# First attention: a tile's value products in small pieces among the next tile's units, two places for probabilities, context loaded later

## What is computed

```python
qkv = x @ w_qkv                        # 16 heads of 64
q, k = rope(q), rope(k)
scores = q @ k.T / 8                   # (16, 512, 512), causal
kerple = -softplus(log_p) * log1p(softplus(log_a) * |i - j|)
hidden = gelu(concat(scores, kerple over heads) @ w1 + b1)      # 32 -> 32
scores = scores + kerple + hidden @ w2 + b2                     # 32 -> 16
weights = softmax(causal(scores))
out = (weights @ v) @ w_o
```

## Time and profile before

| | |
|---|---|
| median of 3 runs (lowest to highest) | 4395.63 us (4395.07 to 4396.11) |
| the profiled execution | 4399.94 us |
| its span, first to last instruction | 4398.2 us |
| PE / DVE / ACT busy in the span | 87% / 56% / 38% |
| share of the chain that ended last: PE / DVE / ACT | 66% / 16% / 7% |
| mean granted TensorE clock | 0.934 of full |

### The profile page before, as it was taken

One profiled execution on the slowest core, in us unless ns is written; L12 is line 12 of the kernel. 1 busy time (PEld: TensorE's weight loads), 2 busy tenths in 40 slices (PEclk: granted clock), 3 DMA queues, 4 the chain that ended last, 5 costly groups with the idle time before them and its releaser, 6 DMA issues.

```text
span 4398.2 us, 57319 instructions
## 1 busy us (share of the span) xinstructions
PE 3843.8 (87%) x21938; PEld 1843.6 (42%) x21938; DVE 2449.9 (56%) x6073; ACT 1681.6 (38%) x2508; POOL 152.0 (3%) x168
## 2 busy tenths in 40 slices
PE   5778888999977888899987798889998879888999
PEld 2342444345434244435533424443553442443355
DVE  5457566742356756673236575657324667665632
ACT  2644433431264542352136354235113636422511
POOL 1000020000000001000000001100000000200000
PEclk9998999999999998899998999889999889988999
DMA  5213002122421201202241210120315121012031
GB/s 191 96 31 60 17 18 48 22 87 75 129 75 37 45 17 42 45 1 101 65 161 44 41 36 17 42 45 1 105 61 161 49 45 27 18 42 45 1 112 59
DMA packets 134702, 254.40 MB, mean 58 GB/s; under 512 B 23268, under 2 KB 82660, under 8 KB 128996
## 3 DMA queue, kind: packets, MB, share of 16 engines
q1 hardware_dynamic: 134408, 250.50, 20.0%
HBM read 156.04 MB, written 44.04 MB: 45 GB/s over the span
## 4 chain that ended last, share of the span: by engine, by line
PE 66%; DVE 16%; ACT 7%; SPq 5%; issue 3%; DMA 2%; POOL 0%; DVEq 0%; POOLq 0%; ACTq 0%
PE ps L1207 11%; PE ps L578 7%; PE ps L1225 5%; DVE mx L732 5%; PE ps L561 5%; SPq L429 5%; PE ps L506 4%; PE ps L1543 3%; DVE ps L729 3%; PE ps L1461 3%; PE ps L402 3%; ACT a_X L1616 2%; PE ps L566 2%; PE ps L1485 2%; DMA a_fin<-scores 2%
## 5 line engine op out<-in xcount | busy, mean ns | idle before, releaser
L670 ACT ACTIVATE PT<-ps 128x1024 f32<-128x1024 f32 (+3 forms) x640 | 604.8, 958 | 473.1 <-PE ps L566 243.6
L506 PE MATMUL ps<-KS,QS 96*128 96x512 bf16 (+3 forms) x1280 | 469.3, 406 | 114.6 <-DVE mx L732 53.5
L732 DVE TENSOR_REDUCE mx<-ps 128x1 f32<-128x512 f32 (+3 forms) x768 | 437.8, 619 | 169.0 <-PE ps L506 82.7
L1207 PE MATMUL ps<-xnT,f_w 128*128 128x512 f32 x1088 | 490.9, 595 | 0.0
L561 PE MATMUL ps<-QS,KS 99*128 99x512 bf16 (+2 forms) x1280 | 429.7, 381 | 6.7 <-ACT QS L660 6.2
L729 DVE CUSTOM_DVE_ANT_0 ps<-ps,mneg 128x512 f32<-128x512 f32 x512 | 342.2, 715 | 133.0 <-PE ps L506 131.3
L578 PE MATMUL ps<-PT,VP 128*32 128x512 f32 (+3 forms) x2560 | 386.5, 588 | 14.2 <-ACT OT L681 13.9
L1313 DVE TENSOR_TENSOR f_tm<-f_si,ps 128x512 f32<-128x512 f32 x128 | 88.1, 688 | 493.2 <-ACT f_si L1265 493.1
L1265 ACT ACTIVATE f_si<-ps 128x512 f32<-128x512 f32 x136 | 80.8, 597 | 596.6 <-PE ps L1220 577.5
L506 PEld LDWEIGHTS ps<-KS,QS 96*128 96x128 bf16 x1280 | 131.2, 103 | 414.1 <-DVE mx L732 195.8
L1207 PEld LDWEIGHTS ps<-xnT,f_w 128*128 128x128 f32 x1088 | 206.9, 191 | 204.9 <-issue 198.4
(11 more groups left out here) (266 smaller groups left out, 5416.5 us busy)
## 6 DMA issues: line engine op xcount, KB each, us to landing
f_w<-in_wF SPq DMA_DIRECT2D x136, 384.0 KB, 3.1
scores<-a_fin SPq DMA_DIRECT2D x64, 256.0 KB, 3.0
a_fin<-scores SPq DMA_DIRECT2D x16, 1024.0 KB, 8.5
a_Y<-in_wA SPq DMA_DIRECT2D x5, 3072.0 KB, 14.9
KS<-KP SPq DMA_DIRECT2D x240, 64.0 KB, 2.5
scores<-a_fin SPq DMA_DIRECT2D x64, 192.0 KB, 3.0
a_fin<-scores SPq DMA_DIRECT2D x16, 768.0 KB, 4.3
a_fin<-scores SPq DMA_DIRECT2D x24, 512.0 KB, 3.6
```

The lines of the kernel that those rows point to most:

```text
L506: last = nc.tensor.matmul(o, m["QS"][0:KR, h, i * P:(i + 1) * P], m["KS"][0:KR, h, f:f + w], start=True, stop=not c.causal)
L670: nc.scalar.activation(m["PT"][:, mp % 2, j % 2, :, 0:w], ps[:, b0:b0 + 2, 0:w], ACT.Exp, scale=HD ** -0.5).then_inc(g("exp"), 1)
L732: nc.vector.tensor_reduce(m["mx"][:, h % 2, i, f // BANK:f // BANK + 1], ps[:, k % 2, 0:w], AX.X, ALU.max, negate=True).then_inc(g("slot_f ...
L1207: last = nc.tensor.matmul(ps[:, 2 * v + e % 2, :], m["w"][:, e % NRING, (2 * v + k) * P:(2 * v + k + 1) * P], xnT[:, k, :], start=(k == 0) ...
```

## The change

- `values` of a tile come in pieces: 8 pieces of 2 heads for tiles 3 and 2, 4 pieces of 4 heads for tile 1, 2 pieces of 8 heads for tile 0.
- They are placed later. The first is one step behind the last turns of the tile. Tile 3 has one piece in each of the steps 12, 13, 14, 15 and two in each of 16, 17; tile 2 two in each of 18, 19, 20, 21; tile 1 two in each of 22, 23; tile 0 two in step 24. Within a step the pieces stand ahead of the turns. `out` moves from step 13 to 18 for tile 3, from 19 to 22 for tile 2, from 23 to 24 for tile 1, and stays in 25 for tile 0, the first bank use of its step.
- The turns of the next tile run meanwhile, so `PT` gets a second place: tiles 3 and 1 keep `a_Y`; tiles 2 and 0 use the upper half of `a_X` for the key blocks 0 and 1, and the block 2 of tile 2 goes into `ctxT`.
- So `ctxT` can't be loaded ahead: SP loads it behind the last load of scores, when the last value piece of tile 2 is done (step 21).

```diff
-        M2["PT"] = M2["Y"][:, :].rearrange("p (j q c) -> p j q c", j=NI, q=AQ)
+        even = M2["Y"][:, :].rearrange("p (j q c) -> p j q c", j=NI, q=AQ)
+        odd = M2["X"][:, 8 * BANK:16 * BANK].rearrange("p (j q c) -> p j q c", j=2, q=AQ)
+        third = ctxT[:, :, :].rearrange("p k (q c) -> p (k q) c", c=P)
+        M2["PT"] = {(i, j): even[:, j] if i % 2 else (odd[:, j] if j < 2 else third) for i in range(NI) for j in range(i + 1)}
...
+        V_HEADS = [4, 2, 1, 1]
+        VALUES_AT = [[0, 0], [0, 0, 1, 1], [0, 0, 1, 1, 2, 2, 3, 3], [0, 1, 2, 3, 4, 4, 5, 5]]
...
-                    after[units[-1]].append(("values", i, 0))
-                    after[units[-1] + 1].append(("values", i, 1))
-                    after[units[-1] + 2].append(("out", i, 0))
+                    at = [units[-1] + 1 + d for d in VALUES_AT[i]]
+                    for v, u in enumerate(at):
+                        after[u].append(("values", i, v))
+                    after[at[-1] + 1].append(("out", i, 0))
...
+            sp.wait_ge(g("bank_mm"), BANK_OF["values", 2, len(VALUES_AT[2]) - 1] + 1)
+            load_ctx(sp, b)
...
-                for t, j, e in itertools.product(range(4), range(i + 1), range(2)):
-                    h, r = 8 * f + 2 * t + e, AW * e
+                for t, j, e in itertools.product(range(V_HEADS[i]), range(i + 1), range(2)):
+                    h, r = 2 * (V_HEADS[i] * v + t) + e, AW * e
...
-                        nc.vector.tensor_copy(m["OT"][:, 4 * b:4 * b + 4, :], bank.rearrange("p (t q) -> p t q", t=4)).then_inc(g("bank_up"), 1)
+                        nt = V_HEADS[a]
+                        nc.vector.tensor_copy(m["OT"][:, nt * b:nt * b + nt, :], bank[:, 0:nt * P].rearrange("p (t q) -> p t q", t=nt)).then_inc(g("bank_up"), 1)
...
-                sp.dma_start(ctxT[:, :, :], io["ctxT"][bass.ds(b, 1), :, :].rearrange("o (k p) j -> p (o k) j", p=P)).then_inc(ctx_loaded, 16)
```

More of the change, by code:

```diff
@@ L1410, in decoder, with load_ctx, a_sp @@
         first_loaded = ctx.enter_context(nc.semaphore("first_loaded"))
-        def a_sp(sp, _, n, st):
+        def load_ctx(sp, b):
+            sp.dma_start(ctxT[:, :, :], io["ctxT"][bass.ds(b, 1), :, :].rearrange("o (k p) j -> p (o k) j", p=P)).then_inc(ctx_loaded, 16)
+        def a_sp(sp, b, n, st):
             g = lambda s: sm["A", s]
@@ L1535, in turn, with weighted @@
                 last.then_inc(g("bank_mm"), 1)
-            def weighted(y, i, f):
+            def weighted(y, i, v):
                 pe.wait_ge(g("bank_up"), BANK_OF["turn", TILE_END[i], len(A_TURNS[TILE_END[i]]) - 1] + 1)
-                for t, j, e in itertools.product(range(4), range(i + 1), range(2)):
-                    h, r = 8 * f + 2 * t + e, AW * e
-                    rhs = m["PT"][:, j, :, :].rearrange("p q (u h) -> p h q u", h=AH)[:, h]
+                for t, j, e in itertools.product(range(V_HEADS[i]), range(i + 1), range(2)):
+                    h, r = 2 * (V_HEADS[i] * v + t) + e, AW * e
+                    rhs = m["PT"][i, j].rearrange("p q (u h) -> p h q u", h=AH)[:, h]
                     o = ps[r:r + AW, A_TURN + y % 2, t * P:(t + 1) * P].rearrange("p (q u) -> p q u", u=AU)
@@ L1546, in out_product @@
             def out_product(y, i):
-                pe.wait_ge(g("bank_up"), BANK_OF["values", i, 1] + 1)
+                pe.wait_ge(g("bank_up"), BANK_OF["values", i, len(VALUES_AT[i]) - 1] + 1)
                 for t in range(KT_A):
@@ L1685, in a_dve @@
                         first = CHUNKS[a][1] + q
-                        nc.vector.tensor_copy(m["PT"][:, j, first:first + 4, :], bank.rearrange("p (q c) -> p q c", q=4)).then_inc(g("bank_up"), 1)
+                        nc.vector.tensor_copy(m["PT"][CHUNKS[a][0], j][:, first:first + 4, :], bank.rearrange("p (q c) -> p q c", q=4)).then_inc(g("bank_up"), 1)
                     elif what == "values":
-                        nc.vector.tensor_copy(m["OT"][:, 4 * b:4 * b + 4, :], bank.rearrange("p (t q) -> p t q", t=4)).then_inc(g("bank_up"), 1)
+                        nt = V_HEADS[a]
+                        nc.vector.tensor_copy(m["OT"][:, nt * b:nt * b + nt, :], bank[:, 0:nt * P].rearrange("p (t q) -> p t q", t=nt)).then_inc(g("bank_up"), 1)
                     else:
```

## The result

The changed kernel takes 4382.85 us in the median (4372.98 to 4398.19) against 4393.64 (4381.43 to 4402.5) of the kernel before on the same chips: a ratio of 0.9975, 95% interval 0.9967 to 0.9983, 10.8 us less. Forecast were 22.4 us less. Two further measurements of the same pair gave 0.9987 (0.9974 to 1.0001) and 0.9975 (0.9962 to 0.9989).

The account below looks back on a forecast made before the run. PE's idle time and clock were taken as what can move: (a) 23.1 + (b) 53.8 + (c) 41.3 = 118.2 against 123.8 us, 22.4 less in four rounds. Forecast 4373 us, range 4350 to 4396.

Parts of the forecast that it names:

- (a): Steps 12 to 15, gelu 12 to the last turn of step 15: 23.1 us a round, a gain of 12.4.
- (b): Steps 16 to 20, to the start of up(21): 53.8 us a round against 53.5, five exposed loads, no gain.
- five times 0.85: Half-clock charge behind the five exposed loads: 1.3 x 0.85 for each of four, 4.4 us, and 1.1 on up(21).
- (c): From up(21) to the end of stage A: 41.3 us a round against 36.8, a loss of 4.5.
- The sum of stage A: Gelu 12 to the end of stage A, (a) + (b) + (c): 118.2 us against 123.8, 5.6 a round less.
- The edits at nothing: Late load of ctxT, DVE's 14 additional copies a round and other places of PT: claimed to cost nothing.
- A clock that stays up: Rival: PE's clock stays up or halves only under value products; 111.4 us a round, 4346 in all, chance 0.17.
- DVE holding up the banks: Rival: the third bank use waits for DVE in steps 12 to 21; no gain, 4395 us, chance 0.16.
- The slow rival: Half clock on whole ups behind exposed loads and in steps 12 to 16; 8.8 us a round slower, 4431, chance 0.13.

Follow-up runs that it names:

- the dummies: Changed kernel with 10 dummy matmuls of PE added behind the last matmul of stage A in each round; 4389.9 us, 0.9991 to the kernel before.

## Why the prediction was right, and where it was too large

The measured time is in the range and the sign is right; the size is half of the forecast in the first measurement, and 6.2 and 6.8 us by the medians of the other two.

- **(a), 23.1 forecast.** 22.5, 22.5 and 23.1 in three profiles. Gelu 13 follows gelu 12 by 3.25 us (197.51 and 194.26), as said, and ACT just fits under PE. The 12.4 called a gain are mostly work that left (a): PE's busy time fell by 10.4 there, its idle time by 2.1. The sum over the three parts has that right.
- **(b), 53.8 forecast.** 54.5, 54.4, 55.0. The sign of the trade was right: the pieces ahead of the turns expose five loads instead of three, 14.6 us of idle time against 9.3 before, while the waits for ACT and DVE in (b), 6.0 us, nearly went; PE's idle time in (b) is 15.0 us against 15.2. The five stretches from turn to `up` sum to 19.3 to 19.7; forecast were 19.4, and that this fits is in part luck: 4.4 to 4.7 for chunk 9, which I had no row of a wait for and took as 3.5, and 3.8 to 3.9 for tile 0, taken as 4.5. The prediction had named loads outside 3.5 to 4.5 as a sign of being wrong; chunk 9's is one. The five `up`s at 13.5 to 14.4 against 10.0 with a busy PE give 3.5 to 4.4 us of clock; forecast were 5.5 with `up(21)`, over `up`s and turns. Two small slips stand in the working: half clock also followed an idle stretch of 2.14 us (round 4, ahead of `up(18)`), not only 2.3 and more, and five stretches instead of five times 0.85 make 1.0 us a round, not 0.8. The Trainium skill's rule on a loop that waits for a transfer in each turn ("TensorE: Matmul & The Clock Gate", "HAM oscillation — how this bites in real kernels") holds for `up(17)`, 3.4 us in the mean of the rounds, and in part for the others, 2.3 to 3.0 for 1.9 to 2.0 at full clock: of the sixty `up`s of the three profiles, 20 ran at full clock, 10 wholly at half clock and 30 partly.
- **(c), 41.3 forecast.** 41.1, 41.7, 42.0, with 10.2 us more of busy PE than before and 4.6 less idle. The 2.50 us of PE behind DVE ahead of the turns of step 21 stand where they were put.
- **The sum of stage A, 118.2 forecast against 123.8.** 118.9 against 123.3 in three profiles each: 4.4 us a round instead of 5.6.
- **The edits at nothing.** Right as far as the intervals tell: the late context (0.9994) and the splitting (0.9995).
- **The rivals.** A clock that stays up (4346) did not come by itself. DVE holding up the banks was no more than 0.3 us at a time in steps 12 to 20 of this order, but it was the very thing that took the load's place once the turns stood ahead. The slow rival needed half clock on three `up`s of steps 12 to 16; (a) ran at 1.00 throughout in 8 of 12 rounds, and at half clock for 3.4 to 6.8 us in the others.

What made it too large is a term that isn't written there: the sum let everything outside the stretch stand as it was. Stages B to F differ by up to 24 us between profiles of the same code, and in this pair went 10 us against the gain (3277.4 to 3287.5). In three pairs it is 5.4 us against 17.7. A second mis-sizing sits beside it: the kernel before was taken from one profile, whose stretch was 0.5 us a round above the mean of three. The means of the profiled spans are 4396.1 and 4381.7, 14.3 apart; 10.8 is what the medians of the first measurement give. That the changed kernel meets the clock in stages B to F in a worse way in most executions is what the mean clocks of 82 and 24 executions speak for; by which path isn't shown. In stage B the moment of entry is the likely one, since a delay brought three of four rounds back.

So over the stretch the change took away 12.0 us a round of waits for DVE and ACT, and gave back 5.2 of waits for loads and 2.5 of PE's busy time (means of three profiles each). The first of these is shown: work that had stood behind the turns was put ahead of them, and releasing the loads earlier took the waits away. Of the second, the `up`s hold 1.5, the value products 1.2 (0.119 us a record in the spread pieces, 0.116 before) and the `out`s 1.0, while the transposes take 1.1 less.

## What to carry to other kernels

When work is moved into gaps, look at what the step it is put ahead of releases: here the last turn frees a buffer and starts a load, and with the pieces ahead of it, instead of behind, five loads a round were exposed instead of three; releasing four of them earlier was worth over five times what the change gained. When work is only moved, compare busy and idle time over the whole stretch: (a) alone showed 12.5 us of gain, of which 10.4 was work that came back later. When a wait is taken away, the order in which the next engine serves its queue is the next suspect. And a gain of 0.3% in one stage of a program should be checked over several profiles of the other stages, and over the mean clock of many executions, before it is believed or missed.

## What the runs showed of the hardware

- Identical code took one of few times: stage E 207.4, 209.1 or 211.2 us (three of 56 rounds near 209.8), stage B 182.7 to 183.6 or 184.0 to 185.7. In round 2 the two times of stage B are told apart by the clock (0.60 against 0.76 over 20 us). Entered 1.8 us later, behind the dummies, stage B took 183.3 us in three of four rounds, against 184 us or more in most rounds of the changed kernel.
- Over fourteen profiles, stages B to F were 0.34 us longer for each us of them at half clock (369 to 443 us of some 3275, correlation 0.92).
- The 1 MB load of the context landed 4.9 us after its issue when it ran alone at the end of the stage, and 8.2 behind the load of stage B's weights.
- Value products of 64 weight columns and 128 moving columns hardly feel the clock: 7.31 us for 64 records of which 2.2 us ran at 0.5, and 7.62 to 7.66 for 64 at full clock. In the small pieces of the changed kernel a record took 113 to 128 ns at full clock and 114 to 129 where a part ran at half.
- A DVE copy of 128x128 from PSUM takes 0.28 us in the changed kernel, the value read off the slope between the two widths of the earlier trace rows.
